# A message-passing layer on one core: TensorE takes candidates and scatters in twos, VectorE adds the windows up five chunks behind

## The reference

```
h   = relu(layernorm(x))                       # 6250 x 64
msg = relu(h[src] + edge_attr)                 # 206250 x 64: a gather and an add
agg = segment_sum(msg, dst, 6250)              # a scatter-add
out = x + (relu((h + agg) @ W1 + b1) @ W2 + b2)
```

## Time and profile before

| | |
|---|---|
| median of three runs | 1508.2 us |
| profiled execution, its own time | 1508.06 us |
| its span, first to last instruction | 1506.2 us |
| PE busy | 1464.1 us, 97% |
| POOL busy | 1133.5 us, 75% |
| DVE busy | 1010.3 us, 67% |
| ACT busy | 143.9 us, 10% |

### The profile page before, as it was taken

One profiled execution on the slowest core, in us unless ns is written; L12 is line 12 of the kernel. 1 busy time (PEld: TensorE's weight loads), 2 busy tenths in 40 slices (PEclk: granted clock), 3 DMA queues, 4 the chain that ended last, 5 costly groups with the idle time before them and its releaser, 6 DMA issues.

```text
span 1506.2 us, 29191 instructions
## 1 busy us (share of the span) xinstructions
PE 1464.1 (97%) x10219; PEld 792.9 (53%) x10219; DVE 1010.3 (67%) x2296; ACT 143.9 (10%) x171; POOL 1133.5 (75%) x1139
## 2 busy tenths in 40 slices
PE   2999999999999999999999999999999999999997
PEld 1555555555555555555555555555555555555554
DVE  8866676666766666666666666666666766677544
ACT  5100000000000000000000000000000000001111
POOL 5777777777777777777777777777777777777774
PEclk9999999999999999999999999999999999999997
DMA  6132232232332222223222233232232322323231
GB/s 228 38 85 85 56 85 75 65 85 56 84 85 56 85 58 83 85 56 85 70 70 85 56 85 85 56 85 57 83 85 56 85 69 72 85 56 86 60 101 35
DMA packets 67162, 115.17 MB, mean 76 GB/s; under 512 B 29810, under 2 KB 32882, under 8 KB 67010
## 3 DMA queue, kind: packets, MB, share of 16 engines
q1 hardware_dynamic: 30130, 75.86, 15.2%
q0 software_dynamic: 36000, 36.94, 12.0%
q10 hardware_dynamic: 1008, 2.06, 0.4%
HBM read 111.43 MB, written 3.34 MB: 76 GB/s over the span
## 4 chain that ended last, share of the span: by engine, by line
PE 91%; POOL 5%; issue 2%; DVE 2%; ACT 1%; DMA 0%; POOLq 0%; DVEq 0%
PE ps_cand L957 83%; PE ps L383 7%; POOL gath L347 5%; ACT agg L608 1%; DVE row_sum L702 0%; DVE row_ssq L709 0%; ACT table_hi L602 0%; PE ps L421 0%; DVE iota_pf L666 0%; DVE xh L392 0%; PE ps L406 0%; DVE xh L718 0%; PE ps L934 0%; DMA gath<-h_table,idx_pair 0%; DVE onehot L660 0%
## 5 line engine op out<-in xcount | busy, mean ns | idle before, releaser
L347 POOL DMA_INDIRECT gath<-h_table,idx_pair x1125 | 1117.9, 994 | 349.2 <-issue 312.7
L957 PE MATMUL ps_cand<-table_hi,keyhot 128*128 128x448 f16 x3409 | 1204.4, 353 | 0.0
L957 PE MATMUL ps_cand<-table_lo,keyhot 128*128 128x448 f16 x3409 | 1203.2, 353 | 0.0
L779 DVE TENSOR_TENSOR picked<-ps_cand,cand_mask 128x448 f32<-128x448 f32 x487 | 290.7, 615 | 474.4 <-PE ps_cand L957 474.2
L957 PEld LDWEIGHTS ps_cand<-table_hi,keyhot 128*128 128x128 f16 x3409 | 334.0, 98 | 313.2 <-issue 5.8
L957 PEld LDWEIGHTS ps_cand<-table_lo,keyhot 128*128 128x128 f16 x3409 | 334.0, 98 | 300.8 <-issue 1.7
L786 DVE TENSOR_REDUCE gath<-picked 128x64 f32<-128x448 f32 x487 | 266.5, 609 | 0.0
L687 DVE TENSOR_SCALAR keyhot<-key_pair,key_iota 128x512 f16<-128x512 f16 (+2 forms) x868 | 260.7, 369 | 0.1
L389 ACT ACTIVATE msg<-xh 128x832 f32<-128x832 f32 x124 | 111.5, 899 | 1333.2 <-DVE xh L805 1333.2
L383 PEld LDWEIGHTS ps<-onehot,msg 128*64 128x64 f32 x3224 | 112.3, 139 | 46.0 <-issue 46.0
L383 PE MATMUL ps<-onehot,msg 128*64 128x20 f32 (+1 forms) x3224 | 129.7, 221 | 0.0
(11 more groups left out here) (57 smaller groups left out, 83.9 us busy)
## 6 DMA issues: line engine op xcount, KB each, us to landing
edge_pair<-edges_t SPq DMA_DIRECT2D x62, 832.0 KB, 4.4
gath<-h_table,idx_pair POOLq DMA_INDIRECT x1125, 2.4
key_pair<-key_table SPq DMA_DIRECT2D x62, 256.0 KB
h_table<-xh SPq DMA_DIRECT2D x7, 224.0 KB, 2.0
x_b<-x_cols SPq DMA_DIRECT2D x1, 1568.0 KB
out<-x_sq SPq DMA_DIRECT2D x6, 224.0 KB, 5.4
idx_pair<-src_t SPq DMA_DIRECT2D x62, 13.0 KB, 1.7
xh<-x_rows ACTq DMA_DIRECT2D x4, 224.0 KB, 5.4
```

What stands on the lines that cost most here:

```text
L347: nc.gpsimd.indirect_dma_start(out=gath[u][:, r, :], out_offset=None, in_=h_table, in_offset=bass.IndirectOffsetOnAxis(ap=idx[u][:, r:r + ...
L779: nc.vector.tensor_tensor(picked[i][:, :, :], ps_cand[buf][:, 0:D * CAND].rearrange("p (d b) -> p d b", b=CAND), mask.to_broadcast([P, D, ...
L957: last = nc.tensor.matmul(bank[:, 0:D * CAND], keyhot[u % 2][:, a, i * P:(i + 1) * P], half[:, a, :, :].rearrange("p d b -> p (d b)"), sta ...
```

## The change

On PE, in the loop of turns 1 to 27, the four slots of a turn are taken in two pairs. For a pair of chunks c and c + 1 (c even), PE does the candidates of c, the candidates of c + 1, the scatter of c - 3 and the scatter of c - 2. Before, the order was candidates of c, scatter of c - 3, candidates of c + 1, scatter of c - 2. The written-out turns at both ends keep the old order on PE.

On DVE, `chunk` accumulates chunk c - 5 instead of c - 4, and does so after the comparison of the keys and ahead of `combine`, not at the end. This holds for the loop and for the last three turns. Turn 1 is now written out on DVE, since its first slot has nothing to accumulate yet. One accumulation more (chunk 119) is left for the end, and stands ahead of the loads of the last four window bases. `back` is rewritten so that it can go back more than four chunks. That the scatter's tiles lie on two halves of the output partitions holds before and after.

```diff
         def back(t, u, n):
-            return (t, u - n) if u >= n else (t - 1, u - n + SLOTS)
+            turns = (n - u + SLOTS - 1) // SLOTS
+            return t - turns, u - n + turns * SLOTS
...
-            def chunk(t, u, since=4, between=None):
+            def chunk(t, u, since=5, between=None):
                 if since > 0:
                     compare_keys(t, u)
+                if since >= 5:
+                    accumulate(*back(t, u, 5))
                 if since >= 1:
                     combine(*back(t, u, 1), between)
                 if since >= 2:
                     sum_edges(*back(t, u, 2))
-                if since >= 4:
-                    accumulate(*back(t, u, 4))
...
-            with dve.Fori(1, EARLY_TURNS[0]) as t:
+            for u in range(SLOTS):
+                chunk(1, u, since=4 + u)
+            with dve.Fori(2, EARLY_TURNS[0]) as t:
                 for u in range(SLOTS):
                     chunk(t, u)
...
             combine(TURNS - 1, SLOTS - 1)
+            accumulate(TURNS - 2, SLOTS - 1)
             bases = [window_base(TURNS - 1, u) for u in range(SLOTS)]
...
             with pe.Fori(1, EARLY_TURNS[0]) as t:
-                for u in range(SLOTS):
+                for u in range(0, SLOTS, 2):
                     candidates(t, u)
+                    candidates(t, u + 1)
                     scatter_chunk(*back(t, u, 3))
+                    scatter_chunk(*back(t, u, 2))
```

## The result

The changed kernel took 1515.63 us, the median of five runs (1510.41 to 1518.49), the kernel before 1507.06 us in five runs beside them (1505.30 to 1509.61). The ratio is 1.0051, with a 95% interval of 1.0037 to 1.0065: slower by half a per cent, and the interval leaves out 1. The profiled execution is the fastest of the five, 1510.41 us, with a span of 1508.6.

What follows compares the result with a forecast made beforehand. PE alone was taken to set the pace. Per pair -0.24 us saved and +0.30 us waited, times 54, gave +3.2 us; with +0.7 us of tail, +3.9 on 1508.06 made 1512.0 us, range 1504 to 1517.

Steps and rivals of the forecast that it cites:

- slower as the likeliest sign: Sign for the whole kernel: slower 0.50, same 0.36, faster 0.14, with 1505.2 to 1511.2 us counted as no change.
- PE sets the pace, and has no slack: In the loop PE alone sets 11.66 us a chunk, and a new wait of PE costs its full length.
- Saved by the order, 0.24 us a pair, 13.0 in all: On PE in the loop, pairing candidates and scatters saves 0.24 us a pair, 13.0 us over 54 pairs.
- The chain, 1.05 us: From first scatter's end through accumulation and mask to the next pair's candidates: 1.05 us against 0.75 us of cover.
- the bounds of 0.14 and 0.42: On DVE, the step from accumulation to mask lies between 0.14 and 0.42 us; 0.25 was taken.
- The stall, 0.30 us a pair: PE stands 0.30 us a pair for the first mask before the next candidates, 0.19 to 0.47 by the bounds.
- The accumulation's waits, 54 of 5.4 us: On DVE the accumulation waits 54 times for the scatter, about 5.4 us each, costing nothing except where it ends.
- The end, +0.7 us: Behind the last chunk, one more load and accumulation on DVE cost 0.5 us, plus 0.2 for later gathers.
- the rival that has POOL as the bound: In the loop both `sum_edges` of a pair hold a gather, up to 0.9 us each; 1520 us and up, chance 0.06.
- no new wait: Rival: the mask is done while the second scatter runs, so PE never waits; 1495.8 us, chance 0.06.
- The lower bound of the chain: Rival: accumulation to mask takes 0.14 us, PE waits 0.19 a pair; 1506.1 us, range 1503 to 1509, chance 0.26.

Runs made afterwards that it cites:

- VectorE's part alone: Accumulation of c - 5 between comparison and combine on DVE, PE in the old order, against the kernel before: 1507.10 us, ratio 1.0007.

## Why the prediction was right, step by step

The forecast was 1512.0 us, with slower as the likeliest sign at 0.50; the median is 1515.63, inside the range and near its upper end. The mechanism was right, and is shown by the versions with and without the wait. The size was less well hit: the forecast had the change at +3.9 us, the medians say +8.6 (+5.6 to +9.8 by the interval), and the traces account for +5.7 of it. Its steps:

- **PE sets the pace, and has no slack.** Right. The loop's stretch takes 1315.33 us in two kernels with the old order on PE and 1301.83 in three with the new order and no wait.
- **Saved by the order, 0.24 us a pair, 13.0 in all.** Nearly: 13.50 us, 0.25 a pair. The candidates of the second chunk follow at 0.19 us, and the second scatter adds 0.82.
- **The chain, 1.05 us.** Measured 1.09. The hand-over to the accumulation is 0.14 (predicted 0.13), accumulation to mask 0.27 (0.25), mask 0.64 (0.62), to PE 0.04 (0.05). The value taken between the bounds of 0.14 and 0.42 was the right choice. It is two steps of the sequencer behind a waiting instruction, as argued from the earlier trace rows: 0.04 and 0.09, with 0.14 for hand-overs. Where the accumulation waits for nothing, the mask follows after 0.13 (704.82 to 704.95, VectorE's part alone). The Trainium skill (Advanced Engine Details and Errata, section Network/Comms) has 50 to 100 ns for reading a semaphore; the hand-overs of 0.03 to 0.05 us in the chain above lie at or under it.
- **The stall, 0.30 us a pair.** Measured 0.34 in the mean, by the gaps of 0.49 and 0.51 us against a bare 0.155. This is the mis-sized term: 54 x 0.34 = 18.6 us where 16.2 were predicted. Three of the four links of the chain were one or two hundredths too short, 0.04 in all, and 54 of them make 2.4 us. With the 0.5 us more that the order saves, the loop costs +5.1 us, not +3.2. The profile puts 14.8 us of it down to the mask as PE's idle time, where some 12 were forecast.
- **The accumulation's waits, 54 of 5.4 us.** Right: 263.5 us in 50 waits and 32.1 in 6. Two of them, 3.9 us, stand at the end of the kernel; the 54 of the loop are 5.40 us each in the mean. That they cost nothing except where they end is shown by the version with the accumulation behind the first mask, which keeps them (4.84 us each in the mean) and is 1.3% faster than the changed kernel.
- **The end, +0.7 us.** Measured +0.55. The last-but-one `sum_edges` starts 2.54 us after its one-hot instead of 1.72, as forecast some 0.8 later: DVE is idle for 1.99 us behind the accumulation, where it was idle for 1.30. The last one follows it after 2.09 us instead of 2.36, since it now waits for the relu and no longer for the last gather. The 0.2 us that were added for a later last gather did not come: POOL was further ahead.
- **What was not foreseen** is a saving on POOL. Before, a gather that starts inside `sum_edges` is held, and POOL falls into step with DVE. A held gather ends 0.81 to 0.82 us behind that `sum_edges`, however early in it it started, in the traces of both kernels. That fits a hold until `sum_edges` ends; no run here takes the two apart. So far the rival that has POOL as the bound read the rows rightly. In the changed kernel POOL gets ahead bit by bit, and in the second half of the loop ends its gathers 32 to 34 us ahead of their `sum_edges` instead of 14. The rival that had it fall behind was wrong in sign. It changes nothing, as nobody waits for POOL. In the two versions without the stall the lead is about 14 us again; why, was not looked into.

The three rivals: "no new wait" was right about the price of having none. It gave 1495.8 us, and the two versions that only remove the wait took 1493.14 and 1496.04. The lower bound of the chain is out by the 0.27 us. POOL is not the bound in any of the kernels on the faster chips: in none of their loops does DVE wait for a gather.

The forecast's sum stood on the time of one execution, though, and the last 110 us of such an execution spread by more than the effect (7.8 us between two profiles of the changed kernel). The median lies 3.6 us above 1512. Of this 1.9 come from the loop. The rest fits that spread, but the median run itself was not profiled. That the number fell inside the range is in part luck: another 1.4 us of it would have been outside.

## What to carry to other kernels

When a bulk of work is put in front of an engine that sets the pace, follow the first thing that it needs afterwards back through the other engine's list: an instruction that waits holds everything behind it, needed or not. Here moving the accumulation behind a single mask turned +0.4% into -0.85%. A long idle time in the trace says nothing about its price; only what stands behind it, and when that is wanted, does.

## What was unexpected of the hardware

- A wait of PE of 2.2 to 2.6 us mostly costs about 1.7 us more in granted clock (behind 50 of 54); a wait of 0.3 us costs none, 53 times.
- Behind the loop, where PE waits for the dense layers, the clock falls in some executions and not in others of the same kernel: 88.9 against 93.9 us for one stretch.
- On one chip before took 1877 us instead of 1507, with idle time of PE that the profile puts down to nothing it sees, often in pieces of 0.72 us. The expectations behind those four runs call it instructions that come late; no trace shows that. There the ratio of the changed kernel was 1.13 instead of 1.005. The three versions with two scatters in a row were hit hardest (1.10 to 1.14 against 1.02).
